# Four B products of the last chunk on GpSimd, and the last two state sums half by half, in a fused graph-convolution, Mamba and LSTM kernel

## The reference

```python
def _mamba(h, ...):                       # D_INNER 256, D_STATE 16
    xz = h @ w_in                         # xc and z
    u = silu(causal_conv4(xc) + conv_b)
    dbc = u @ w_xp                        # dt (8), B (16), C (16) for each row
    dt = softplus(dbc[:, :8] @ w_dt + b_dt)
    dA = exp(dt[:, :, None] * A[None])
    dBu = dt[:, :, None] * B[:, None, :] * u[:, :, None]
    # scan over the rows: hst = dAt * hst + dBut; y = hst @ Ct
    y = ys + u * D_skip
    return (y * silu(z)) @ w_out

h = layernorm(relu(adj @ layernorm(x) @ gcn_w + gcn_b))
x = x + _mamba(h)
x = x + ffn(layernorm(x))                 # an LSTM over the 8192 rows, then prefix and suffix sums
```

## Time and profile before

| | |
|---|---|
| median of 3 runs | 1590.91 us (1589.63 to 1592.43) |
| the profiled execution | 1590.84 us, span 1588.80 us |
| iterations 0 to 16 | to about 1258 us |
| iteration 17 on VectorE | 1257.93 to 1319.05 us |
| iteration 18 | to about 1335.7 us |
| LSTM and output | to 1588.8 us |
| busy share of the span | TensorE 95%, VectorE 86%, GpSimd 71%, ScalarE 65% |

### The profile page before, as it was taken

One profiled execution on the slowest core, in us unless ns is written; L12 is line 12 of the kernel. 1 busy time (PEld: TensorE's weight loads), 2 busy tenths in 40 slices (PEclk: granted clock), 3 DMA queues, 4 the chain that ended last, 5 costly groups with the idle time before them and its releaser, 6 DMA issues. The chain is left out here.

```text
span 1588.8 us, 17874 instructions
## 1 busy us (share of the span) xinstructions
PE 1507.8 (95%) x4975; PEld 770.8 (49%) x4975; DVE 1368.8 (86%) x1623; ACT 1024.9 (65%) x2179; POOL 1123.5 (71%) x536
## 2 busy tenths in 40 slices
PE   8999999999999999999999999999997888999994
PEld 3444434444444444444444444444432335999993
DVE  7405999999999999999999999999999896667998
ACT  3254757666676767676758576666767656776772
POOL 0325989898989898989989898989898861001221
PEclk9999999999999999999999999999998899999997
DMA  9867767676776767666777766667642423000002
GB/s 367 330 247 266 259 228 252 246 249 247 252 249 239 265 231 260 243 238 238 255 259 246 255 245 247 251 243 255 245 171 63 158 72 119 0 0 1 0 0 106
DMA packets 64955, 321.64 MB, mean 202 GB/s; under 512 B 6988, under 2 KB 7040, under 8 KB 31989
## 3 DMA queue, kind: packets, MB, share of 16 engines
q1 hardware_dynamic: 54001, 301.43, 52.6%
q10 hardware_dynamic: 10884, 19.41, 3.8%
HBM read 308.49 MB, written 12.32 MB: 202 GB/s over the span
## 5 line engine op out<-in xcount | busy, mean ns | idle before, releaser
L605 PE MATMUL bank<-ring,xh 128*128 128x512 f32 x2048 | 956.9, 594 | 14.0 <-DVE xh L1197 8.2
L1313 DVE TENSOR_TENSOR_SCAN work<-bank,hstate,work 128x512 f32<-128x512 f32 x512 | 627.7, 1267 | 20.5 <-ACT bank L900 15.7
L605 PEld LDWEIGHTS bank<-ring,xh 128*128 128x128 f32 x2048 | 388.1, 190 | 465.7 <-issue 423.4
L1082 POOL TENSOR_TENSOR work<-work 128x1024 f32<-128x1024 f32 x210 | 495.4, 2359 | 85.5 <-DVE work L1262 77.1
L900 ACT ACTIVATE bank<-work,a_neg 128x512 f32<-128x512 f32 x512 | 344.6, 686 | 250.5 <-DVE work L1313 247.1
L1254 DVE TENSOR_TENSOR work<-work,bank 128x1024 f32<-128x1024 f32 x256 | 309.8, 1215 | 63.3 <-POOL work L1058 54.4
L1262 DVE TENSOR_TENSOR work<-work,bank 128x1024 f32<-128x1024 f32 x168 | 201.0, 1196 | 20.2 <-POOL work L1082 20.2
L499 PE MATMUL bank<-bc_parts,sel 96*128 96x512 bf16 x425 | 163.4, 385 | 20.2 <-DVE work L1254 19.3
L1158 POOL TENSOR_TENSOR work<-work 128x256 f32 x32 | 28.6, 894 | 215.5 <-ACT work L961 215.5
L494 PE MATMUL bank<-work,w_sb 128*128 128x512 f32 (+2 forms) x352 | 176.3, 598 | 1.3 <-DVE work L1243 0.7
L1027 POOL TENSOR_TENSOR work<-work 128x1024 f32<-128x1024 f32 x48 | 113.5, 2364 | 19.0 <-ACT work L783 18.9
(11 more groups left out here) (152 smaller groups left out, 1574.4 us busy)
## 6 DMA issues: line engine op xcount, KB each, us to landing
ring<-adj_t SPq DMA_DIRECT2D x256, 1024.0 KB, 5.4
xh<-c_scratch SPq DMA_DIRECT2D x31, 256.0 KB, 3.3
work<-c_scratch ACTq DMA_DIRECT2D x28, 256.0 KB, 5.6
c_two<-c_scratch ACTq DMA_DIRECT2D x28, 256.0 KB, 5.0
xh<-x_rows SPq DMA_DIRECT2D x16, 256.0 KB, 7.0
work<-x_t SPq DMA_DIRECT2D x16, 256.0 KB, 5.2
x_scratch<-work ACTq DMA_DIRECT2D x16, 256.0 KB, 3.6
work<-x_scratch SPq DMA_DIRECT2D x1, 4096.0 KB, 13.2
```

The costliest lines, as they stand in the source:

```text
L605: last = nc.tensor.matmul(mixed[:, :], xn[:, j, :], a, start=(j == 0), stop=(j == BLK - 1))
L1082: nc.gpsimd.tensor_tensor(out=acc, in0=hc[0] if n == 1 else acc, in1=hc[n % 2], op=ALU.add).then_inc(y_added, 1)
L1313: nc.vector.tensor_tensor_scan(hb[s % 2][:, h, :], da[h], dbu[s % 2][:, h, :], hstate[:, HV * s + h:HV * s + h + 1], ALU.mult, ALU.add).th ...
```

## The change

In iteration 17 the B products of states 5, 8, 11 and 14 are made by GpSimd. ScalarE stores the B rows of chunk 15 beside its C rows (c_scratch gets 32 rows for each chunk, C in the upper half), SyncE loads those four rows, broadcast, ahead of load_rows and of the C rows, and GpSimd multiplies them with dtu behind its C product of two states earlier, into dt[0], dtu[0] or acc. TensorE leaves out their four spreads, VectorE the four products, and scans 5, 8, 11 and 14 wait for GpSimd's. In iteration 18 TensorE adds states 14 and 15 into the first half's bank, then into the second half's, once both C products are there, and VectorE waits for each half alone. ScalarE evicts o products 12 and 13 both in slot 14.

```diff
+POOL_DBU = (5, 8, 11, 14)
...
+def dbu_count(cs, n):
+
+    return DS * cs + sum(1 for m in range(n + 1) if cs < NC - 1 or m not in POOL_DBU)
...
-    c_dram = nc.dram_tensor("c_scratch", (NC, DS, CH), F32, kind="Internal").ap()
+    c_dram = nc.dram_tensor("c_scratch", (NC, 2 * DS, CH), F32, kind="Internal").ap()
...
+        b_late = [xh[:, (2 + LATE + i) * CH:(3 + LATE + i) * CH] for i in range(len(POOL_DBU))]
+        dbu_late = [dt[0], dtu[0], acc]
...
                     if k == NC + 1:
+                        for i, n in enumerate(POOL_DBU):
+                            sp.dma_start(b_late[i], c_dram[NC - 1, n:n + 1, :].broadcast_to([P, CH])).then_inc(b_late_in[i], 16)
                         load_rows()
...
-                    if s < DS - 2 and scan:
-                        wait(pe, dbu_done, DS * cs + (s + 1))
+                    if s < DS - 2 and scan and not (k == NC + 1 and s + 2 in POOL_DBU):
+                        wait(pe, dbu_done, dbu_count(cs, s))
...
+                def last_sums():
+
+                    for h in range(HV):
+                        for n in (DS - 2, DS - 1):
+                            last = nc.tensor.matmul(y_bank[h][:, :], ident, hc[n % 2][:, h, :], start=False, stop=(n == DS - 1))
+                        last.then_inc(y_half_done, 1)
...
+                    if k == NC + 2:
+                        return
...
+                        if k == NC + 2 and s == 1:
+                            last_sums()
...
-                        act.dma_start(c_dram[k - 1], dbc[DS:2 * DS, :]).then_inc(c_stored, 16)
+                        first = 0 if k == NC else DS
+                        act.dma_start(c_dram[k - 1, first:2 * DS], dbc[first:2 * DS, :]).then_inc(c_stored, 16)
...
-                    if k == NC + 2 and s in (14, 15):
-                        save_o(O_SHARED + 3 + s - 14)
+                    if k == NC + 2 and s == 14:
+                        for c in (O_SHARED + 3, O_SHARED + 4):
+                            save_o(c)
...
+                def make_dbu(n):
+                    i = POOL_DBU.index(n)
+                    pool.wait_ge(b_late_in[i], 16)
+                    pool.wait_ge(scan_done, HV * DS * (NC - 1) + (HV * (POOL_DBU[i - 3] + 1) if i >= 3 else 0))
+                    nc.gpsimd.tensor_tensor(out=dbu_late[i % 3], in0=dtu[par], in1=b_late[i].unsqueeze(1).broadcast_to([P, HV, CH]),
+                                            op=ALU.mult).then_inc(late_dbu, 1)
...
+                        if k == NC + 1 and s + 2 in POOL_DBU:
+                            make_dbu(s + 2)
...
-                        dve.wait_ge(y_summed, DS * (k - NC))
+                        if k == NC + 1:
+                            dve.wait_ge(y_summed, DS)
                         for h in range(HV):
+                            if k == NC + 2:
+                                dve.wait_ge(y_half_done, h + 1)
...
-                    if s < DS - 1:
+                    on_pool = k == NC + 1 and s in POOL_DBU
+                    if s < DS - 1 and not (k == NC + 1 and s + 1 in POOL_DBU):
                         make_dbu(s + 1)
...
-                            dve.wait_ge(dbu_done, DS * cs + s + 1)
+                            if on_pool:
+                                dve.wait_ge(late_dbu, POOL_DBU.index(s) + 1)
+                            else:
+                                dve.wait_ge(dbu_done, dbu_count(cs, s))
```

More of the change, by code:

```diff
@@ L320, in build @@
         skip_ready, y_skip, y_ready = sems("skip_ready y_skip y_ready")
-        y_half_sum, y_half, last_hc = sems("y_half_sum y_half last_hc")
+        y_half_sum, y_half, last_hc, y_half_done = sems("y_half_sum y_half last_hc y_half_done")
+        late_dbu = sem("late_dbu")
+        b_late_in = [sem(f"b_late_in{i}") for i in range(len(POOL_DBU))]
         x1_stored, psq_ready, prstd_ready = sems("x1_stored psq_ready prstd_ready")
@@ L405, in step @@
                             sp.wait_ge(pool_hc_done, len(POOL_HC) * (NC - 2) + i - LATE + 1)
-                        sp.dma_start(c_late[i % LATE], c_dram[k - 2, n:n + 1, :].broadcast_to([P, CH])).then_inc(c_late_in[i % LATE], 16)
+                        sp.dma_start(c_late[i % LATE], c_dram[k - 2, DS + n:DS + n + 1, :].broadcast_to([P, CH])).then_inc(c_late_in[i % LATE], 16)
                 if adj:
@@ L876, in load_c @@
                     wait(act, pool_hc_done, hc_count(cs, n, True) - 2)
-                    act.dma_start(c_rows[b], c_dram[cs, n:n + 1, :].broadcast_to([P, CH])).then_inc(c_row_in[b], 16)
+                    act.dma_start(c_rows[b], c_dram[cs, DS + n:DS + n + 1, :].broadcast_to([P, CH])).then_inc(c_row_in[b], 16)
                 def save_state(c, n):
@@ L1251, in make_dbu @@
                 def make_dbu(n):
-                    dve.wait_ge(b_ready, DS * cs + n + 1)
+                    dve.wait_ge(b_ready, dbu_count(cs, n))
                     wait(dve, scan_done, HV * (DS * cs + n - 1) if isinstance(cs, int) else HV * DS * cs + HV * (n - 1))
@@ L1309, in step @@
                         if h == 0:
-                            dve.wait_ge(dbu_done, DS * cs + s + 1)
+                            if on_pool:
+                                dve.wait_ge(late_dbu, POOL_DBU.index(s) + 1)
+                            else:
+                                dve.wait_ge(dbu_done, dbu_count(cs, s))
                             wait(dve, state_saved, DS * cs + (s - 1))
                             wait_hc(dve, cs, s - 2)
-                        nc.vector.tensor_tensor_scan(hb[s % 2][:, h, :], da[h], dbu[s % 2][:, h, :],
+                        nc.vector.tensor_tensor_scan(hb[s % 2][:, h, :], da[h],
+                                                     (dbu_late[POOL_DBU.index(s) % 3] if on_pool else dbu[s % 2])[:, h, :],
                                                      hstate[:, HV * s + h:HV * s + h + 1],
```

## The result

The kernel with the change takes 1594.32 us (median of 14 runs, 1591.91 to 1596.24), the kernel before beside it 1591.34 us (14 runs, 1589.63 to 1595.39). The ratio is 1.0017, interval 1.0009 to 1.0024: **2.7 us slower, between 1.4 and 3.8**. A second measurement gave 1.0014 (1.0005 to 1.0023). The forecast had been 2.4 us slower.

What follows compares the result with a forecast made beforehand. VectorE was taken to bound the step; waiting for GpSimd's chain puts the last C product +2.5 us later, half-by-half sums give -0.5, the clock +0.4: +2.4 on 1590.91, so 1593.3 us, range 1589.5 to 1597.0.

Steps and rivals of the forecast that it cites:

- The chain: Iteration 17: scans 5, 8, 11 and 14 wait for GpSimd's B products, queued behind late C products: +2.1, +2.7, +3.3, +3.0 us.
- The clock: TensorE in iteration 17: idle time lowers the granted clock, 1.45 us a spell on the chain; +0.4 us net taken.
- The spell at step 3: Lower clock from the o product at 1273.47 to C product 3; if missing, scan 5 starts about 1.1 us earlier.
- The last C product: End of iteration 17: scan 15 ends at 1322.0, so the last C product starts near 1322.05, +2.5 us.
- The half-by-half sums: Tail: TensorE's order puts the second output product 6.2 us behind the last C product's end, not 6.71: 0.5 us gained.
- Edits at nothing: Moved o gate evictions (0.5 us if cover is gone) and row transfers ahead of the 3,328 KB load: no cost.
- A: Rival: GpSimd is in time, VectorE gains 5.2 us and the end 0.5, giving 1585.2 us; chance 0.07.
- B: Rival: clock falls in nearly every cycle, on the path; two spells +4.9, three +6.4, 1595.8 to 1597.3 us; chance 0.20.
- C: Rival: GpSimd's added work slows VectorE through shared SBUF interfaces; at most 0.5 us over 20 scans; no separate chance.
- D: Rival: the row transfers delay the 3,328 KB load past its reader, +1 to +2 us on top, 1595; chance 0.03.

Runs made afterwards that it cites:

- The early placement: The change with GpSimd's B products each two steps earlier, behind C product n-4 instead of n-2, against the kernel before: ratio 0.9983, iteration 17 61.87 us.
- the turned order: The change with TensorE's state sums ahead of the o products in steps 2 to 10 of iteration 17, against the kernel before: ratio 0.9982.
- the kernel with fillers: The whole change plus eight unread spreads on TensorE at steps 3, 6, 9 and 12 of iteration 17, against the kernel before: ratio 0.9985.
- before again: The kernel before, unchanged, measured against itself for scatter and a second trace: ratio 0.9998 (0.9989 to 1.0006), iteration 17 62.56 us.
- half-by-half alone: The change without GpSimd's B products, keeping half-by-half last sums and both evictions in one slot, against the kernel before: ratio 0.9985, tail 15.01 us.
- its filler version: Half-by-half sums without GpSimd's B products, plus eight unread spreads in step 3 of iteration 17, against the kernel before: ratio 0.9987.
- the two moves together: The change with GpSimd's B products two steps earlier and state sums ahead of o products in steps 2 to 10, against the kernel before: ratio 0.9941.

## Why the prediction was right

**The chain (+2.1, +2.7, +3.3, +3.0).** From scan 2 to scan 5 the change took 13.21 us for 11.08 before: +2.13, forecast +2.1. The pitch from scan 5 to scan 8 was 11.68, forecast 11.7; from 8 to 11 it was 13.38 in this trace, 11.68 in the second one (where the pitch before it was 13.20). From 11 to 14 it was 11.05, forecast 11.1, for 11.46 before. The early placement (no scan waits for a B product) and the turned order (pitch 11.05) show the two links, late C product and product behind it.

**The clock (+0.4 net).** Right in kind, too small in size. I priced a spell at 1.45; the pitches show 1.70 and 1.52. Both traces of the change have one such spell among scans 5 to 11, and both have one more at sum 11, which I hadn't counted in the sum. The spell at step 3, which the chain's +2.1 holds and which might have been missing, was there in both. From scan 2 to the last C product the kernel with fillers takes 51.31 us for 54.80 with the change: 3.5 less, of which 1.2 is the spell at step 3 (1.1 in the forecast), 1.7 the one ahead of scan 11 and 0.6 the one at sum 11. The bare chain is then 1.3 us over before (50.03), near the forecast's 2.5 less 1.1. So against the first trace of before the term was +2.3 in the place of +0.4. Against the second, which has a spell of its own on the path and takes 51.77 us, it was +0.5: the forecast had put no spell on the path of the kernel before.

**The last C product (+2.5).** Scan 2 to the last C product is 54.80 us for 50.03: +4.8. Of it +2.1 is scan 5, +0.6 + 2.3 the two pitches, -0.4 the one to scan 14, and +0.15 the end (5.48 for 5.33), where the forecast had 0.5 less than before. The step that failed there is the assumption that nothing stood between scans 14 and 15: scan 15 waits for C product 13, which GpSimd began only at 1319.60, because sum 11 ran at the lower clock; it cost 0.48 us. In the table the difference is 3.96, as the first two steps of iteration 17 happened to take 0.8 us less after the change; against before again it is 3.0.

**The half-by-half sums (-0.5).** Measured -0.63, by TensorE's order as argued: the second output product starts near 1332.1, 6.2 us behind the last C product's end, as forecast, for 6.71 before. VectorE's next addition, behind it, starts 7.29 us after that end for 7.92, which is the whole 0.63.

**Edits at nothing.** The evictions cost and gave nothing that lasts (15.65 for 15.64). The 3,328 KB load was issued at 1244.88 and landed 15.9 us later, at 1260.8, 6.2 us ahead of o product 0 at 1266.95 (the forecast had counted some 8, to the scans of that step); no wait for a transfer is in the trace.

**The sum, and why it still fitted.** In part by luck. In the first pair of traces iteration 17 is 4.77 us longer from scan 2 on, for a forecast of +2.9, and the tail 0.63 shorter for 0.5. The spans differ by 2.7 all the same, because three things that the forecast doesn't have add up to -1.44: the first steps of iteration 17 took 0.81 less (VectorE waits 0.71 us for a state sum there in the trace of before), the part behind the tail 1.73 less, and iteration 17 began 1.10 later. In the second pair the iteration's +3.0, the tail's -0.6 and -1.8 behind it leave 0.6, and with the iteration beginning 0.7 earlier the spans are 1590.8 and 1590.9 us, while the ratio over many executions is 1.0014. So the 2.4 us of the forecast agree with the medians, and no pair of traces adds up to them by the terms of the forecast alone.

The 1.73 us are one spell of the lower clock more or less in the LSTM, behind the idle time between its two rounds (2.04 us on TensorE in both traces). Windows of before, then of after, at that place:

```profile
1444.00:1450.00 6.00, 6.00 (x41) 5.95 (x40) 2.80 (x9) 3.61 (x15) 0.00 (x0) 0.74 0.01 3
```

```profile
1448.00:1454.00 6.00, 6.00 (x54) 5.95 (x53) 3.75 (x11) 4.63 (x20) 0.00 (x0) 1.00 0.01 4
```

**The rivals.** A fell (VectorE idle at every one of the four scans). B was half true: in iteration 17 two spells counted, not three, but the kernel's median, 1594.3, stayed under the 1595.8 that B had for two. C fell: the scans still take 2.45 us a pair beside GpSimd's added work, and the pitches without a spell are those of the sum. The contention that the Trainium skill names ("GPSIMD Engine Reference", 1. Specifications) doesn't show here, but what rival C took from there is said of VectorE instructions with two SBUF inputs. VectorE's scans and B products read one of their two streams from a PSUM bank, so these runs don't test it. D fell.

**What stays open.** By ratio, half-by-half alone is 2.4 us (1.0 to 3.8) faster and its filler version 2.1 (0.8 to 3.5), while iteration 17 and the tail in their traces explain 0.5 or less; the kernels with fillers, early products or turned sums are likewise better than their stretches. From the LSTM's third step up to its spell all fourteen traces agree within 0.1 us, counted from the tail's end. The spell itself is there in all four without the half-by-half sums and in three of the ten with them. That would be worth about 1 us on average, but 14 single traces don't settle it, and nothing in these runs says why the one should follow from the other.

## What to carry to other kernels

Before work moves to an engine with idle time, ask at which end of its wait the idle time lies: a product queued behind one that is always released late is late too, and here two steps earlier in the same queue took the whole loss away (2.7 us slower than before, then 2.7 faster, where half-by-half alone had 2.4). Where an engine's order puts a sum behind a product that waits for a third engine, try the two the other way round; the two moves together made iteration 17 8.2 us shorter than with the change, where each alone gave 3.5 to 3.7. Idle time on TensorE can have a second price, the lower clock in what follows, in some executions; here it cost nothing where VectorE's own work set the pace, and 0.5 to 1.7 us a spell where the waiting chain did.

## What was not expected of the hardware

Eight matmuls that nobody reads (1.89 us together), put into each of the idle stretches of 2.2 to 3.1 us ahead of needed products, came with an iteration 2.7 us shorter: the granted clock was 1.00 throughout, and the products behind them ran at full speed (o product 1.10 for 1.94 us, sum 1.88 for 2.77). And the same idle time of 2.48 us before the same product was followed by the upper clock in one execution (1.12 us) and by the lower in another (1.83 us): a spell is a matter of the execution, not of the program alone. Nor did the longer wait bring the lower clock: in one trace of the change 3.13 us of idle time left the product and the sum behind it at 1.10 and 1.88 us, and 2.17 us did not (1.94 and 2.77).
